# Gated state and first residual kept in the projection's PSUM tile

## The reference

```python
# first stage, the one that is changed
i, f, g = x @ Wi.T, x @ Wf.T, x @ Wg.T
a = exp(log_sigmoid(f));  b = silu(i) * (1 - a)
h = scan(h[t] = a[t] * h[t-1] + b[t])
xg = h * silu(g)
y = xg * rsqrt(mean(xg**2) + EPS) * w_norm
x = layernorm(x + y @ Wo.T)
# second stage: a weighted running average over time (wkv) of ctx with keys x, then layernorm(x + ...)
# third stage: gated MLP (512 -> 1408 -> 512) with operands rounded to 8-bit steps, then layernorm(x + ...)
```

## Time and profile before

| | us |
|---|---|
| median of 3 runs | 489.2 (488.76 to 492.02) |
| span of the profiled execution, first to last instruction | 485.3 |
| that execution's own time | not recorded beside its span |

### The profile page before, as it was taken

The page is one execution under the profiler, slowest core; times in us unless marked ns, Lnnn a source line. Parts: engine busy times, 40 slices in busy tenths (PEclk is TensorE's granted clock), DMA queues, the critical chain, the costliest instruction groups (busy, mean ns, idle before and its releaser), DMA issues.

```text
span 485.3 us, 7425 instructions
## 1 busy us (share of the span) xinstructions
PE 376.6 (78%) x2484; PEld 285.2 (59%) x2484; DVE 426.4 (88%) x705; ACT 290.8 (60%) x374; POOL 277.5 (57%) x249
## 2 busy tenths in 40 slices
PE   5977972997098995899598977898689959556782
PEld 4965972886064973588365865396459836223331
DVE  3897599848999999989998999799998999999983
ACT  4766673493446965387547864586538654854752
POOL 4546574706836754586365935384558636763643
PEclk8997895999589997999989989899799988976998
DMA  8849441460110010201002010301020101000001
GB/s 312 300 171 141 149 156 53 132 108 35 50 37 1 0 66 1 102 8 54 14 22 88 1 66 0 109 0 65 0 105 3 65 0 42 24 0 22 22 24 66
DMA packets 13340, 31.70 MB, mean 65 GB/s; under 512 B 4864, under 2 KB 4864, under 8 KB 13312
## 3 DMA queue, kind: packets, MB, share of 16 engines
q1 hardware_dynamic: 13312, 31.35, 20.4%
HBM read 27.14 MB, written 4.21 MB: 65 GB/s over the span
## 4 chain that ended last, share of the span: by engine, by line
DVE 45%; PE 17%; issue 16%; POOL 9%; DMA 8%; ACT 4%; DVEq 1%; POOLq 0%; SPq 0%; ACTq 0%
DVE q_state L1427 7%; PE proj_ps L455 6%; PE slot_ps L557 6%; DVE p_state L1439 6%; DVE hid_max L1534 4%; DMA ring<-w_gate_up_dram 3%; POOL q_state L1173 2%; DVE ring L1522 2%; DVE ring L1525 2%; DVE num L1447 2%; DVE row_max L1591 2%; DVE inp L1359 2%; POOL ring L1189 2%; POOL z L1194 2%; PE slot_ps L590 2%
## 5 line engine op out<-in xcount | busy, mean ns | idle before, releaser
L557 PE MATMUL slot_ps<-w1q,xqT 128*128 128x512 bf16 (+1 forms) x384 | 88.2, 382 | 20.6 <-DVE z L1567 12.9
L1189 POOL TENSOR_TENSOR ring<-ring 128x512 f32<-128x512 f32 (+1 forms) x48 | 66.2, 1386 | 18.8 <-ACT ring L867 18.7
L557 PEld LDWEIGHTS slot_ps<-w1q,xqT 128*128 128x128 bf16 x384 | 37.8, 102 | 63.8 <-issue 14.5
L455 PE MATMUL proj_ps<-x_high,proj_high 128*128 128x256 f32 x384 | 64.3, 289 | 5.0 <-DVE proj_low L1350 1.9
L455 PE MATMUL proj_ps<-x_high,proj_low 128*128 128x256 f32 x384 | 61.5, 282 | 0.0
L455 PE MATMUL proj_ps<-x_low,proj_high 128*128 128x256 f32 x384 | 61.1, 281 | 0.0
L455 PEld LDWEIGHTS proj_ps<-x_high,proj_high 128*128 128x128 f32 x384 | 52.9, 189 | 7.8 <-issue 6.0
L867 ACT ACTIVATE ring<-ring,zero_bias,x_scale 128x512 f32<-128x512 f32 (+1 forms) x48 | 36.9, 772 | 31.7 <-DVE ring L1522 31.6
L455 PEld LDWEIGHTS proj_ps<-x_high,proj_low 128*128 128x128 f32 x384 | 52.6, 190 | 0.0
L455 PEld LDWEIGHTS proj_ps<-x_low,proj_high 128*128 128x128 f32 x384 | 52.4, 190 | 0.0
L523 PE MATMUL turn_ps<-identity,num 128*128 128x128 f32 x64 | 14.5, 391 | 44.2 <-DVE num L1465 44.2
(11 more groups left out here) (115 smaller groups left out, 904.7 us busy)
## 6 DMA issues: line engine op xcount, KB each, us to landing
ring<-w_gate_up_dram SPq DMA_DIRECT2D x11, 512.0 KB, 4.9
forget<-xT_dram SPq DMA_DIRECT2D x8, 512.0 KB, 3.3
x_sb<-x_dram SPq DMA_DIRECT2D x8, 512.0 KB, 3.4
c_sb<-cT_dram SPq DMA_DIRECT2D x8, 512.0 KB, 4.9
out_dram<-z SPq DMA_DIRECT2D x16, 256.0 KB, 2.1
ring<-w_down_dram SPq DMA_DIRECT2D x4, 704.0 KB, 5.0
x<-wfT_dram SPq DMA_DIRECT2D x2, 512.0 KB, 5.0
x<-woT_dram SPq DMA_DIRECT2D x2, 512.0 KB, 4.6
```

The costliest lines, as they stand in the source:

```text
L455: last = nc.tensor.matmul(out, a, b, start=(i == 0), stop=(i == len(terms) - 1))
L557: last = nc.tensor.matmul(slot_ps[:, s, half * 512:half * 512 + width], xqT[:, par, d, t * P:(t + 1) * P], w1q[:, d, half * I + at:half * ...
L1189: nc.gpsimd.tensor_tensor(hid, hid, gate_buf[:, at:at + width], ALU.mult).then_inc(hid_ready, 1)
```

## The change

silu(g) is written back into `proj_ps`, so `gate_feat`, a view of the two banks by feature block, takes the place of `gate`; the gated product, the high and low parts and the squares are taken from there, each in two halves of 512 elements. The residual is added in `proj_ps` too, and statistics and normalisation read it there. `proj_read` now counts four reads per batch (`READS`), not six. No call changes its place in an engine's list, except that ACT's `square` is now part of its `split_states`. The waits that change: `project(b, 0)` and `(b, 1)` wait for x1 of the batch before; `project_out` for both halves and for the squares; DVE's low half h for high half h and squares h; ACT's silu(i) for the last gating and no longer for x1; ACT's silu(g) for nothing but its matmuls.

```diff
+READS = 4
...
-        z1 = inp[:, :, :].rearrange("p (t a) c -> p t (a c)", t=TB)
...
+        gate_feat = proj_ps[:, :, :].rearrange("p k (e t) -> p (k e) t", t=T)
...
                 if k < 2:
-                    wait(pe, z1_ready, b * TB - TB + k + 1)
+                    wait(pe, x1_ready, b * TB - TB + k + 1)
                 else:
-                    pe.wait_ge(proj_read, b * PROJ + k - 1)
+                    pe.wait_ge(proj_read, b * READS + k - 1)
...
-                pe.wait_ge(xg_high_ready, b + 1)
-                pe.wait_ge(xg_low_ready, b + 1)
-                pe.wait_ge(proj_read, b * PROJ + 5 + t)
+                pe.wait_ge(xg_high_ready, 2 * b + 2)
+                pe.wait_ge(xg_low_ready, 2 * b + 2)
+                pe.wait_ge(sq_ready, 2 * b + 2)
...
                 if m == 1:
-                    wait(act, x1_ready, b * TB)
-                if m == 2:
-                    wait(act, sumsq_done, b)
+                    wait(act, xg_ready, 2 * b)
...
                 else:
-                    nc.scalar.activation(dst[:, e, :], src, ACT.Silu,
-                                         bias=zero_bias[:, :]).then_inc(proj_read, 1)
+                    nc.scalar.activation(src, src, ACT.Silu,
+                                         bias=zero_bias[:, :]).then_inc(gate_ready, 1)
...
             def split_states(b):
-                act.wait_ge(xg_ready, b + 1)
-                wait(act, wo_done, b * TB)
-                nc.scalar.activation(xg_high[:, :, :], inp[:, :, :], ACT.Identity,
-                                     bias=zero_bias[:, :]).then_inc(xg_high_ready, 1)
+                for h in range(2):
+                    act.wait_ge(xg_ready, 2 * b + h + 1)
+                    if h == 0:
+                        wait(act, wo_done, b * TB)
+                        wait(act, sumsq_done, b)
+                    nc.scalar.activation(blocks(xg_high, h), blocks(gate_feat, h), ACT.Identity,
+                                         bias=zero_bias[:, :]).then_inc(xg_high_ready, 1)
+                    nc.scalar.activation(blocks(sq, h), blocks(gate_feat, h), ACT.Square,
+                                         bias=zero_bias[:, :]).then_inc(sq_ready, 1)
...
             def gating(b):
                 dve.wait_ge(h_ready, b + 1)
-                dve.wait_ge(proj_read, b * PROJ + 6)
-                nc.vector.tensor_tensor(flat(inp), flat(inp), flat(gate),
-                                        ALU.mult).then_inc(xg_ready, 1)
+                for h in range(2):
+                    dve.wait_ge(gate_ready, 2 * b + h + 1)
+                    nc.vector.tensor_tensor(flat_half(gate_feat, h), flat_half(inp, h),
+                                            flat_half(gate_feat, h),
+                                            ALU.mult).then_inc(xg_ready, 1)
...
             def split_states(b):
-                dve.wait_ge(xg_high_ready, b + 1)
-                nc.vector.tensor_tensor(flat(xg_low), flat(inp), flat(xg_high).bitcast(F32),
-                                        ALU.subtract).then_inc(xg_low_ready, 1)
+                for h in range(2):
+                    dve.wait_ge(xg_high_ready, 2 * b + h + 1)
+                    dve.wait_ge(sq_ready, 2 * b + h + 1)
+                    nc.vector.tensor_tensor(flat_half(xg_low, h), flat_half(gate_feat, h),
+                                            flat_half(xg_high, h).bitcast(F32),
+                                            ALU.subtract).then_inc(xg_low_ready, 1)
...
-                nc.vector.scalar_tensor_tensor(z1[:, t, :], proj_ps[:, t, :], rms[:, t:t + 1],
+                nc.vector.scalar_tensor_tensor(proj_ps[:, t, :], proj_ps[:, t, :], rms[:, t:t + 1],
                                                x_sb[:, t, :], ALU.mult,
                                                ALU.add).then_inc(z1_ready, 1)
...
-                    last = nc.vector.bn_stats(stats1[:, t, :], z1[:, t, :])
+                    last = nc.vector.bn_stats(stats1[:, t, :], proj_ps[:, t, :])
...
-                    nc.vector.tensor_scalar(x1[:, t, :], z1[:, t, :], mv1[:, t, 0:1],
+                    nc.vector.tensor_scalar(x1[:, t, :], proj_ps[:, t, :], mv1[:, t, 0:1],
                                             rstd1[:, t:t + 1], ALU.subtract,
                                             ALU.mult).then_inc(x1_ready, 1)
```

More of the change, by code:

```diff
@@ L249, in decoder_layer @@
         proj_read = sem("proj_read")
+        gate_ready = sem("gate_ready")
         forget_ready = sem("forget_ready")
@@ L761, in read_projection @@
                 if m == 1:
-                    wait(act, x1_ready, b * TB)
-                if m == 2:
-                    wait(act, sumsq_done, b)
+                    wait(act, xg_ready, 2 * b)
                 src = proj_ps[:, k % 2, :].rearrange("p (e t) -> p e t", e=2)
-                dst = (forget, inp, gate)[m]
                 if m == 0:
-                    nc.scalar.activation(dst[:, e, :], src, ACT.Tanh, bias=zero_bias[:, :],
+                    nc.scalar.activation(forget[:, e, :], src, ACT.Tanh, bias=zero_bias[:, :],
                                          scale=0.5).then_inc(proj_read, 1)
-                else:
-                    nc.scalar.activation(dst[:, e, :], src, ACT.Silu,
-                                         bias=zero_bias[:, :]).then_inc(proj_read, 1)
+                elif m == 1:
+                    nc.scalar.activation(inp[:, e, :], src, ACT.Silu,
+                                         bias=zero_bias[:, :]).then_inc(proj_read, 1)
+                else:
+                    nc.scalar.activation(src, src, ACT.Silu,
+                                         bias=zero_bias[:, :]).then_inc(gate_ready, 1)
             def forget_gate(b):
-                act.wait_ge(proj_read, b * PROJ + 2)
+                act.wait_ge(proj_read, b * READS + 2)
                 nc.scalar.activation(forget[:, :, :], forget[:, :, :], ACT.Identity,
@@ L805, in split_half @@
                 last.then_inc(half_high, 1)
[L807 to L810, removed]
             def exp_past(b, h):
@@ L943, in iteration @@
                 split_states(b + 2)
-                square(b + 2)
                 silu(b, par, 1, [1])
@@ L976, in _ @@
             split_states(0)
-            square(0)
             split_x(1)
@@ L1007, in _ @@
             split_states(1)
-            square(1)
             keep_rows(10)
@@ L1040, in _ @@
             silu(0, 0, 0, [2])
-            square(2)
             round_hidden(0, 0, 0)
@@ L1126, in sum_blocks @@
             def sum_blocks(b):
-                pool.wait_ge(sq_ready, b + 1)
+                pool.wait_ge(sq_ready, 2 * b + 2)
                 nc.gpsimd.tensor_tensor(sq[:, 0:2, :], sq[:, 0:2, :], sq[:, 2:4, :],
@@ L1357, in weigh_inputs @@
                 dve.wait_ge(forget_ready, b + 1)
-                dve.wait_ge(proj_read, b * PROJ + 4)
+                dve.wait_ge(proj_read, b * READS + 4)
                 nc.vector.scalar_tensor_tensor(flat(inp), flat(forget), 1.0, flat(inp),
```

## The result

The changed kernel takes 498.37 us (median of 4 runs, 497.81 to 499.16), the kernel before 490.58 beside it (4 runs, 488.76 to 492.02). The ratio is 1.0169, with a 95% interval of 1.0123 to 1.0216: about 8.3 us slower, between 6.0 and 10.6. The forecast was 500.5 us, slower by over 1%; in ratio it was 1.023. The profiled execution has a span of 496.9 us against 485.3.

A forecast was written before the change was run, and what follows sets the result against it. VectorE, 45% of the chain, was taken to bound the kernel. 4.6 + 7.1 + 1.4 + 0.1 - 1.9 = +11.3 us on a span of 485.3, with 3.9 carried over, gave 500.5 us; range 495.5 to 505.

The forecast's parts named there:

- First wait: Opening, project(1, 0): TensorE waits for x1, so row 10's load and VectorE come later, +4.6 us, bounds 2.4 to 5.0.
- all six groups at half clock: Opening, project(1, 0): after a longer gap all six matmul groups run at half clock, adding another 0.7 us.
- Second wait: Opening, project(2, 0): waiting for x1 delays mlp_up and sum_values(1, 0), partly hidden by c_sb's load, +7.1 us, bounds 4.9 to 7.5.
- The gated part: Iterations: the low half waits for its squares, +0.28 us in each of five, +1.4 us, bounds 0 to 3.
- The normalisation: normalise_1 out of PSUM isn't stretched beside POOL: -1.35 us in batch 2, -0.6 for the last pair, -1.9, bounds 0 to -3.
- The price of one normalisation: normalise_1 out of PSUM takes 0.69 us, +0.28 a pair, mostly falling into VectorE's waits for TensorE; booked +0.1 us.
- The base: Whole kernel: the run median's 3.9 us above the profiled span of 485.3 is carried over, giving 489.2 us before.
- (a): Opening: one wait is covered, the second costing little and the first 3 to 4 us; 494.7 us, chance 0.12.
- (b): VectorE: PSUM operands cost 0.08 us more in ten instructions a batch, some two thirds unhidden; 504.8 us, chance 0.09.
- (c): Opening: loads end VectorE's gaps, so both TensorE waits vanish in them; not slower, 488.8 us, chance 0.04.

The follow-up runs named there:

- run 1: Kernel before, with only project(b, 0) and (b, 1) waiting for x1 of the batch before, not z1; ratio 1.0213 to the kernel before, +10.4 us.
- run 2: Kernel before, where only project(1, 0) and (1, 1) wait for x1; ratio 1.0099 to the kernel before, +4.8 us.
- run 9: Changed kernel with load_c(1) issued earlier, ahead of load_xT(2); ratio 1.0167 to the kernel before, +8.2 us.
- run 10: Changed kernel as it is, measured once more with more rounds; ratio 1.0163 to the kernel before, +8.0 us.
- run 3: Kernel before, where only project(2, 0) and (2, 1) wait for x1; ratio 1.0154 to the kernel before, +7.5 us.
- run 4: Changed kernel with z1 back in SBUF and its old waits, leaving the gated half alone; ratio 1.0018 to the kernel before, +0.9 us.
- run 8: Kernel before with load_c(1) issued earlier, ahead of load_xT(2); ratio 0.9891 to the kernel before, -5.4 us.
- run 6: Changed kernel with TensorE's opening reordered, calls that need no proj_ps ahead of the projection, ScalarE's list following; ratio 0.9973 to the kernel before, -1.3 us.
- run 11: Changed kernel with the order of run 6 and the earlier load_c(1); ratio 0.9959 to the kernel before, -2.0 us, 486.1 us.
- run 7: Kernel before with the same new opening order as run 6; ratio 1.0017 to the kernel before, +0.8 us.
- run 12: Run 11 with residual_2(b + 1, 0) ahead of the low halves in VectorE's iteration; ratio 1.0025 to the kernel before, +1.2 us.
- run 5: Kernel before with residual, statistics and normalisation in proj_ps and the wait for x1; ratio 1.0201 to the kernel before, +9.8 us.

## Why the prediction was right

The direction, the size and both places were right, and the forecast was 2 us high (3 us by its difference to before, 11.3 against 8.3). By its own steps, each sized from intervals between marks that all kernels share:

- **First wait, +4.6, booked on VectorE's wait for row 10.** The place is right, the size 0.6 too high. The five profiles with this wait and without an order of their own (after, runs 1, 2, 9, 10) have a mean of 54.2 us from batch 0's scan to batch 1's, the four without it (before, runs 3, 4, 8) 49.2. But 1.0 of these 5.0 us lies ahead of `residual_1(0, 0)`, where neither wait can act yet, and the landing of loads moves it. From the start of `residual_1(0, 0)` to batch 1's scan it is 33.9 us (33.5 to 34.3) with the wait and 29.9 (29.2 to 30.6) without: 4.0 us. That is the later start, 4.04 (4.94 us behind the start of the residual, before 0.90) for the 3.93 worked out. The other 0.7 of the term, all six groups at half clock, didn't come: only the first four were slow, as before the change, and the stage took 4.40 us against 4.41. Run 2's +4.8 (2.9 to 6.7) holds both sizes. TensorE's idle time was 6.46 and not 5.8, mostly because it had come to the gap some 0.55 earlier, which changed nothing behind it.
- **Second wait, +7.1, partly hidden by `c_sb`.** Right. With it (after, runs 1, 3, 9, 10) batch 1's scan to batch 2's has a mean of 56.8 us, without it (before, runs 2, 4) 50.2: 6.5 us, and 7.5 by run 3. The start of `sum_values(1, 0)` is where the forecast had it: 9.98 us behind the start of `normalise_1(1)` before (101.24 to 111.22), 16.99 after (108.90 to 125.89), so 7.0 later. That sum then took 2.68 us and not 3.39, which gives 0.7 back; what makes it shorter wasn't tested. Five of six groups ran at half clock, 4.98 us for the 5.1 worked out; TensorE idle 9.46 for "9"; VectorE idle 14.25 for "13 to 14". The 4 us of cover that the load gave show in run 8.
- **The gated part, +1.4, in the iterations.** This step is furthest off, by 1.0 of its 1.4 us, though inside its bounds. The 0.28 is there to the digit (3.57 to 3.85), but an iteration didn't get 0.3 to 0.4 longer. From L1474 to the normalisation of the second stage the same instructions take 4.03 us (361.73 to 365.76) where they took 4.15, since one of them, 0.32 long at 352.72 before, is 0.17 at 364.71; so some of it comes back at once. The rest can't be told from TensorE's clock, which makes 16 matmuls last 5.31 in one iteration and 3.62 in others. From batch 3's scan to batch 7's the kernels with this part (after, runs 4, 6, 9, 10, 11) have a mean of 207.4 us and those without it (before, runs 1 to 3, 7, 8) 207.0, with a scatter of 205.0 to 209.7 in single profiles, so 0.4 can't be told from nothing. Run 4 gives +0.9 (-0.1 to +1.8) for this part.
- **The normalisation, -1.9.** Right as a sum, by luck in how it divides. In batch 2 3.69 became 1.53 (I took 1.3), and the interval from batch 2's scan to batch 3's is 2.0 us shorter in the PSUM forms (50.6, six profiles: after, runs 6, 9 to 12) than in the others (52.5, seven: before, runs 1 to 4, 7, 8), where I had booked 1.35. The last pair went from 1.96 to 1.53, but from batch 7's scan to the end it is 96.1 us (after, runs 6, 9 to 11) against 96.2 (the seven): 0.1, where I had booked 0.6. A pair out of PSUM isn't stretched by the POOL work beside it: all pairs take 1.53 us, in every batch, while out of SBUF six of eight take 1.00 to 1.01 and the two others 3.69 and 1.96; and in runs 6 and 7, at the same place of the same order, it is 1.53 against 3.69. The Trainium skill (SBUF — State Buffer, "Who interferes with whom") had it so, and the trace agrees. The price of one normalisation was sized too low, 806 ns where I took 690, so +0.5 a pair against SBUF's quiet 1.01 and not +0.28; it falls into waits, as I had booked it.
- **What was over.** By these stages the change costs 4.0 + 6.5 + 0.4 - 2.0 - 0.1 = 8.8 us, beside 8.3 and 8.0 measured. So of the forecast's 11.3, 0.6 are too much in each wait, 1.0 in the gated part, and 0.3 too little was given back by the normalisation. These are means over three to seven profiles a side. The runs of single parts are too coarse to divide it: runs 1 and 4 add up to 10.4 + 0.9 = 11.3, which would leave some 3 us for the PSUM residual to give back, run 5 against run 1 gives 0.6, and run 6 against run 7 has the whole PSUM form 2.1 us ahead, where the stages give 2.0 + 0.1 - 0.4 = 1.7; each of these has 2 to 3 us of noise.
- **The base.** I carried 3.9 us over from span to time. Four executions of the changed kernel have 1.75 to 1.86 us between the two (498.65 and 496.9 for the profiled one), so the profiled execution of before, at some 487 us, was faster than any of the four timed beside the changed kernel, and 496.6 against a span of 496.9 agrees in part by luck: 3.8 us of the 11.6 are scatter of loads, 2.55 ahead of batch 0's scan and 1.25 in the landing of row 8, an early one.

The rivals: (a), one wait covered, no; runs 2 and 3 each pay. (b), PSUM dearer, no: of the ten instructions only the two normalisations are dearer, the residual and the statistics stay within 0.01 us of their prices of before, and a gating in two halves takes 1.28 us against 1.22. (c), both waits hidden by loads, no; but its mechanism is real for 4 us of the second, and without `c_sb`'s late load the change would have cost 13.5 us (1.0167 over 0.9891), not 8.

## What to carry to other kernels

When a change lets a buffer be freed later, the cost isn't in the instructions that it adds: look up who takes the buffer next, in every place of the order that is written out by hand, and what stands queued behind that waiting call. Then the same change can cost 8 us or, against the kernel before in the same order, gain some 2, by the place of a few calls on TensorE's list. And ask of a gap that a load ends whether the load could be issued earlier: one moved line took 1.1% off, more than the change and its mended order together; but it counts only where nothing else is as late.

## What was new about the hardware

- VectorE writes PSUM at the price of SBUF: 684 ns for the product and 1.42 us for a pair of residuals, where before they took 682 and 1.41.
- The normalisation with two scalars per partition is the exception: 806 ns out of PSUM, against half of 1.01 us out of SBUF undisturbed. But it was 1.53 a pair in every batch, where the SBUF form was 1.0 in six batches, 3.69 in one and 1.96 in one: the slower source is the one that can be planned with.
- ScalarE's pieces of 512 out of PSUM last 0.69 us, and the next begins 0.56 to 0.59 later, not 0.61. Nothing came of it: the last squares end 3.14 us behind the start of gating and not 3.22, but the second low half starts 3.24 behind it, for a forecast of 3.25. Its wait reads 0.17 and not 0.25 because the row before it ends at 3.07, where I had counted 3.0.
- TensorE was granted its lower level (1.2 of 2.4 GHz) behind all three gaps: 0.50 from 49.22 to 52.60 behind one of 1.86 us in the kernel before (its first row of four still at 1.00), 0.52 for 3.5 us behind 6.46, 0.50 for 4.4 us behind 9.46. So the gap of 6.46 brought four slow groups as the one of 1.86 had, and the one of 9.46 five.
